# Cross attention on one core: turning the probabilities behind the keys, weighing two steps at once, half of the output weights resident

## What is computed

```python
q = (layernorm(x) @ Wq + bq).reshape(b, s, 16, 64)
k = (ctx @ Wk + bk).reshape(b, 2048, 16, 64)
v = (ctx @ Wv + bv).reshape(b, 2048, 16, 64)
logits = einsum('bshd,bShd->bhsS', q, k) / sqrt(64)
weights = softmax(logits, axis=-1)
x = x + einsum('bhsS,bShd->bshd', weights, v).reshape(b, s, 1024) @ Wo + bo
```

## Time and profile before

| | |
|---|---|
| median of 3 runs | 1503.95 us (1503.4 to 1504.15) |
| the profiled execution, its own time | 1505.97 us |
| its span, first to last instruction | 1504.2 us |
| mean granted clock of TensorE | 0.978 |
| busy: PE / DVE / ACT / POOL | 96% / 49% / 33% / 12% |
| cross attention | from 12.35 us, PE's first matmul, to 1190 us |

### The profile page before, as it was taken

One profiled execution on the slowest core, in us unless ns is written; L12 is line 12 of the kernel. 1 busy time (PEld: TensorE's weight loads), 2 busy tenths in 40 slices (PEclk: granted clock), 3 DMA queues, 4 the chain that ended last, 5 costly groups with the idle time before them and its releaser, 6 DMA issues. The chain is left out here.

```text
span 1504.2 us, 22239 instructions
## 1 busy us (share of the span) xinstructions
PE 1449.8 (96%) x8564; PEld 1115.5 (74%) x8564; DVE 739.4 (49%) x1644; ACT 502.8 (33%) x1111; POOL 173.8 (12%) x150
## 2 busy tenths in 40 slices
PE   5999999999999999999999999999999599799999
PEld 4667777777777777777777777777777377588777
DVE  5335433463354336434533463354335555577679
ACT  3115421471153136413421471153124424321111
POOL 3211000130020003101000130020000112100012
PEclk9999999999999999999999999999999897899999
DMA  6511000140010003201000140010011130023300
GB/s 210 174 65 43 19 12 11 39 134 1 11 50 12 11 8 105 61 11 32 18 12 12 39 134 1 11 43 5 4 60 57 16 112 1 26 88 100 96 30 29
DMA packets 44359, 71.50 MB, mean 48 GB/s; under 512 B 8048, under 2 KB 16272, under 8 KB 43616
## 3 DMA queue, kind: packets, MB, share of 16 engines
q1 hardware_dynamic: 42608, 65.04, 14.1%
q0 software_dynamic: 1648, 5.04, 1.1%
HBM read 64.82 MB, written 5.24 MB: 47 GB/s over the span
## 5 line engine op out<-in xcount | busy, mean ns | idle before, releaser
L404 PE MATMUL b_ps<-b_ctxT,wk 128*128 128x512 f32 x1536 | 388.0, 401 | 0.0
L382 PE MATMUL b_ps<-wv,b_ctxT 128*128 128x512 f32 x1536 | 373.2, 401 | 12.4 <-DVE b_ctxT L582 12.4
L382 PEld LDWEIGHTS b_ps<-wv,b_ctxT 128*128 128x128 f32 x1536 | 289.4, 190 | 86.6 <-issue 20.9
L404 PEld LDWEIGHTS b_ps<-b_ctxT,wk 128*128 128x128 f32 x1536 | 279.9, 189 | 58.1 <-issue 1.5
L686 DVE TENSOR_SCALAR_CACHE_REDUCE b_prob<-b_ps 128x512 f32<-128x512 f32 x256 | 166.6, 688 | 309.4 <-PE b_ps L420 309.4
L553 ACT COPY b_pT<-b_ps 128x512 f32<-128x512 f32 x128 | 75.1, 587 | 539.0 <-PE b_ps L433 529.4
L595 DVE COPY b_V<-b_ps 128x512 f32<-128x512 f32 x128 | 88.4, 691 | 250.8 <-PE b_ps L382 250.8
L562 ACT ACTIVATE b_prob<-b_prob,b_negm 128x512 f32<-128x512 f32 x256 | 182.9, 719 | 2.2 <-DVE b_negm L692 2.2
L451 PE MATMUL b_ps<-b_pT,b_V 128*64 128x128 f32 x2048 | 145.5, 279 | 0.3 <-ACT b_pT L553 0.3
L451 PEld LDWEIGHTS b_ps<-b_pT,b_V 128*64 128x64 f32 x2048 | 110.3, 136 | 46.4 <-issue 45.9
L433 PE MATMUL b_ps<-ident,b_prob 128*128 128x128 f32 x1024 | 138.0, 278 | 6.5 <-ACT b_prob L562 6.4
(11 more groups left out here) (201 smaller groups left out, 1249.6 us busy)
## 6 DMA issues: line engine op xcount, KB each, us to landing
stage<-in_ctx SPq DMA_DIRECT2D x64, 256.0 KB, 2.9
stage<-in_Wk SPq DMA_DIRECT2D x30, 256.0 KB, 2.6
stage<-in_Wv SPq DMA_DIRECT2D x28, 256.0 KB, 3.2
b_q<-q_s SPq DMA_DIRECT2D x32, 128.0 KB, 3.0
w_rows<-in_self_w SPq DMA_DIRECT2D x4, 1024.0 KB, 5.0
w_tiles<-in_q_proj SPq DMA_DIRECT2D x16, 256.0 KB, 3.9
w_tiles<-in_k_proj SPq DMA_DIRECT2D x16, 256.0 KB, 3.4
w_tiles<-in_v_proj SPq DMA_DIRECT2D x16, 256.0 KB, 3.4
```

Source lines behind the costliest of these rows:

```text
L382: mm = nc.tensor.matmul(ps[:, bank], ctxT[:, a, k, n * P:(n + 1) * P], wv[:, w, k], start=m == 0, stop=m == len(terms) - 1)
L404: mm = nc.tensor.matmul(ps[:, bank], wk[:, i % 2, w, k], ctxT[:, a, k, s * BANK:(s + 1) * BANK], start=m == 0, stop=m == len(terms) - 1)
```

## The change

Cross attention alone is changed.

- In a step PE does K, then T, then S. W is made in even steps only, for w - 2 and w - 1 (w = t - 6), one behind the other. `pT` has six half buffers instead of two, so a copy waits for the weighing three steps back. The special order of the tail is gone.
- V moves two steps later, O one (within its step it stands where it stood), the value weights are split two steps later, the epilogue comes one step later.
- ACT exponentiates first in a step and copies T after it; DVE does its context chunks ahead of its copy of T.
- `wo` holds half of Wo (4 of 8 row blocks). SP loads the other half each time the group that used it is done: 8 loads of 1 MB in place of one of 2 MB.
- At the start ACT and DVE split the two key weights after x has been transposed instead of before the first value chunks; POOL adds the output bias after the last query product, and the raw tiles lie at other addresses.

```diff
-    LAG_EXP, LAG_WEIGH = 5, 6
+    LAG_EXP, LAG_TURN, LAG_WEIGH = 5, 6, 8
...
-                self.products[half * h + 3 + n // SB].append(("v", h, n))
+                self.products[half * h + 5 + n // SB].append(("v", h, n))
...
-                groups = [(at + 24, 0, 4), (at + 31, 4, 6), (at + 35, 6, 7), (at + 38, 7, 8)]
+                groups = [(at + 25, 0, 4), (at + 32, 4, 6), (at + 36, 6, 7), (at + 39, 7, 8)]
...
-        work += [(half * h - 8 + c, ("wv", h, c)) for h in range(1, self.HALVES) for c in range(C)]
+        work += [(half * h - 6 + c, ("wv", h, c)) for h in range(1, self.HALVES) for c in range(C)]
...
+        loads += [(half * k + (9 if k % 2 == 0 else 10), 2, k, ("wo", k)) for k in range(1, 2 * NB)]
...
-        wo = sb("wo", [P, NP, D])
+        wo = sb("wo", [P, HALF, D])
         pT_at = nc.sbuf_base
-        pT = sb("pT", [P, 2, 4, P])
+        pT = sb("pT", [P, SLOTS, 4, P])
...
+                elif item[0] == "wo":
+                    k = item[1]
+                    sp.wait_ge(o_psum, outs_of(k - 1)[-1] + 1)
+                    sp.dma_start(wo[:], Wo[:, k % 2 * HALF:(k % 2 + 1) * HALF]).then_inc(wo_in, 16)
```

PE:

```diff
             for t in range(LAST + 1):
-                w = t - G.LAG_WEIGH
-                if 0 <= w and t <= TOTAL:
-                    transpose_probs(w)
+                w = t - G.LAG_TURN
                 if t < TOTAL:
                     keys(t)
+                if 0 <= w < TOTAL:
+                    transpose_probs(w)
                 if 1 <= t <= TOTAL:
                     scores(t - 1)
-                if t >= TOTAL and w + 1 < TOTAL:
-                    transpose_probs(w + 1)
-                if 0 <= w < TOTAL:
-                    weigh(w)
+                if w >= 2 and w % 2 == 0:
+                    weigh(w - 2)
+                    weigh(w - 1)
```

ACT and DVE, start and steps:

```diff
-            for n in range(C, len(PRE)):
-                pre_split(n)
...
+                if item[0] == "x":
+                    for n in range(C, len(PRE)):
+                        pre_split(n)
...
-                    if w >= 1:
-                        act.wait_ge(pv_done, 2 * w - 1)
-                    nc.scalar.copy(pT[:, 0], ps[:, TB].rearrange("p (m t) -> p m t", m=4)).then_inc(te_done, 1)
...
+                    if 2 * w >= SLOTS:
+                        act.wait_ge(pv_done, 2 * w - SLOTS + 1)
+                    nc.scalar.copy(pT[:, 2 * w % SLOTS], ps[:, TB].rearrange("p (m t) -> p m t", m=4)).then_inc(te_done, 1)
...
-            for n in range(C, len(PRE)):
-                pre_rest(n)
...
+                    for n in range(C, len(PRE)):
+                        pre_rest(n)
...
+                for item in G.splits[t]:
+                    if item[0] == "ctx" and item[2] % 2 == 0:
+                        chunk_rest(item[1], item[2])
                 if 0 <= w < TOTAL:
```

More of the change, by code:

```diff
@@ L121, in __init__ @@
         self.TOTAL = NB * self.STEPS
-        self.LAST = self.TOTAL + self.LAG_WEIGH
+        self.LAST = self.TOTAL + 7
         self.HALVES = 2 * NB
@@ L186, in cross_attention @@
     QBUFS = 2
+    SLOTS = 6
     with ExitStack() as ctx:
@@ L220, in cross_attention @@
         xnT = at("xnT", [P, C, TOK], prob_at + 4 * C * HW + 4 * NB * D)
-        raw = at("raw", [P, len(PRE), BANK], wo_at)
-        bo_b = at("bo_b", [P, D], wo_at + 4 * len(PRE) * BANK)
+        raw_v = at("raw_v", [P, C, BANK], wo_at)
+        raw_k = at("raw_k", [P, 2, BANK], pT_at + 16 * QBUFS * TOK // 2)
+        bo_b = at("bo_b", [P, D], attn_at)
+        raw = [raw_v[:, c] for c in range(C)] + [raw_k[:, i] for i in range(2)]
         qhi = at("qhi", [P, QBUFS, TOK], pT_at, F32R)
@@ L251, in chunk_lo, with outs_of @@
                 eng.wait_ge(clo_odd, NC // 2 * b + (n + 1) // 2)
+        def outs_of(k):
+            return [n for n, (_, b, first, _) in enumerate(G.outs) if 2 * b + first // HALF == k]
         def weight_lo(eng, item):
@@ L297, in _ @@
             for i in range(2):
-                sp.dma_start(raw[:, C + i], Wk[i]).then_inc(pre_in[C + i], 16)
+                sp.dma_start(raw[C + i], Wk[i]).then_inc(pre_in[C + i], 16)
             for n in range(4, NC):
@@ L303, in _ @@
             sp.wait_ge(pre_lo, len(PRE))
-            sp.wait_ge(xbo_done, NB)
-            sp.dma_start(wo[:], Wo).then_inc(wo_in, 16)
+            sp.dma_start(wo[:], Wo[:, :HALF]).then_inc(wo_in, 16)
             for i in range(2):
@@ L334, in _ @@
                 chunk_rest(0, n)
[L335 to L338, removed]
             for j in range(NP):
@@ L344, in _ @@
                     pool.dma_start(q_s[l, j], src[:, j % QBUFS].bitcast(F32)).then_inc(q_stored[j % QBUFS], 16)
+            pool.wait_ge(bo_in, 16)
+            pool.wait_ge(ln[5], NB)
+            for b in range(NB):
+                nc.gpsimd.tensor_tensor(xs[:, b], xs[:, b], bo_b[:], ALU.add).then_inc(xbo_done, 1)
             for t in range(LAST + 1):
@@ L388, in out_product @@
                 bank = bank_free(item)
-                pe.wait_ge(wo_in, 16)
+                pe.wait_ge(wo_in, 16 * (2 * b + first // HALF + 1))
                 pe.wait_ge(attn_done, NP * b + last)
                 for i in range(first, last):
-                    mm = nc.tensor.matmul(ps[:, bank], attnT[:, i], wo[:, i], start=i == first, stop=i == last - 1)
+                    mm = nc.tensor.matmul(ps[:, bank], attnT[:, i], wo[:, i % HALF], start=i == first, stop=i == last - 1)
                 mm.then_inc(o_psum, 1)
@@ L450, in weigh @@
                         col = (i % HALF * 2 + h) * HD
-                        mm = nc.tensor.matmul(ps[h * HD:(h + 1) * HD, OB, 0:P], V[:, c, col:col + HD], pT[:, half, m],
+                        mm = nc.tensor.matmul(ps[h * HD:(h + 1) * HD, OB, 0:P], V[:, c, col:col + HD], pT[:, (2 * w + half) % SLOTS, m],
                                               start=c == 0, stop=c == NC - 1)
@@ L529, in _ @@
             split_hi(("ctx", 0, 3))
-            for n in range(C, len(PRE)):
-                pre_split(n)
             act.wait_ge(bq_in, 16)
             for item in G.first:
-                if item[0] == "v" and item[2] + 4 < NC:
+                if item[0] == "x":
+                    for n in range(C, len(PRE)):
+                        pre_split(n)
+                elif item[0] == "v" and item[2] + 4 < NC:
                     split_hi(("ctx", 0, item[2] + 4))
@@ L647, in _ @@
             for t in range(LAST + 1):
-                w, e = t - G.LAG_WEIGH, t - 1
-                if w >= SB and w % SB == 0:
+                w, e = t - G.LAG_TURN, t - 1
+                if w > SB and w % SB == 1:
                     i = w // SB - 1
@@ L657, in _ @@
                     dve.wait_ge(o_free, i + 1)
+                    if i == 0:
+                        dve.wait_ge(xbo_done, NB)
                     if i >= NP and i % HALF == 0:
@@ L665, in _ @@
                     dve.wait_ge(t_psum, 2 * w + 2)
-                    if w >= 1:
-                        dve.wait_ge(pv_done, 2 * w)
-                    nc.vector.tensor_copy(pT[:, 1], ps[:, TB + 1].rearrange("p (m t) -> p m t", m=4)).then_inc(to_done, 1)
+                    if 2 * w >= SLOTS:
+                        dve.wait_ge(pv_done, 2 * w - SLOTS + 2)
+                    nc.vector.tensor_copy(pT[:, (2 * w + 1) % SLOTS], ps[:, TB + 1].rearrange("p (m t) -> p m t", m=4)).then_inc(to_done, 1)
                     if s == SB - 1:
@@ L676, in _ @@
                         dve.wait_ge(rinv_done, i + 1)
-                for item in G.splits[t]:
-                    if item[0] == "ctx" and item[2] % 2 == 0:
-                        chunk_rest(item[1], item[2])
                 if 0 <= e < TOTAL:
```

15 lines of the change are left out of this document (8 added, 7 removed).

## The result

The kernel after takes 1487.86 us in the median of 4 runs (1486.79 to 1492.95), the kernel before 1503.68 beside it (4 runs): a ratio of 0.9908 (0.9889 to 0.9926). In a second comparison it took 1489.99 (4 runs), ratio 0.9903 (0.9885 to 0.9920). It is faster by 15 to 16 us by the medians, 14 to 15 by the ratios; 10.7 were forecast, and the range held it.

What follows compares the result with a forecast made beforehand. PE, busy 96% of the span, was taken as the bound. Steps -3.6, tail -6.1, start -4.3 and reload +3.3 sum to -10.7: 1505.97 becomes 1495.3, the median 1493.3 us; range 1486.5 to 1500.

Steps and rivals of the forecast that it cites:

- Steps: Cross attention's step pairs in the new order: .04 us gained 46 times, .13 gained 14 times with V, together 3.6.
- Rival (a): In the steps, all changes of form cost alike, five instead of six per pair: -9.6 us for -3.6, 1487.3; chance 0.10.
- Waits in short steps: In steps without W, S's low keys are ready at 6.87 and wanted at 8.61, 1.7 us left: cost 0.
- rival (d): In every short step S waits for the low keys, as DVE's chain hangs on the previous S: 1517 us; chance 0.05.
- Reload: Context reloaded three times: DVE's chunks now precede T's copy, scores and low keys, making S .95 us late: +3.3 in all.
- Rival (b): Reload costs 9 us instead of 3.3, late copies of T piling up into the next step: 1499; chance 0.13.
- Tail: From K(127) to the last O: 26.0 us instead of 30.38, and one T and W move behind K(127); gain 6.1.
- Start: Before X's third batch, DVE is freed from POOL's additions and key weights: gain 3.5 to 5.7 us, taken as 4.3.
- Rival (c): Both ends only move their waits: tail gains 3, start 1, reload costs 6: 1502.4 us; chance 0.08.
- SP's queue: SP's eight Wo loads wait for an O last in its step; PE uses them 15 steps on: cost 0.

Runs made afterwards that it cites:

- the chunks' order: Kernel after, with DVE subtracting context chunks cast before the key copy between its T copy and scores, the rest behind the low keys: 1486.58 us, ratio 0.9881 to the kernel before.

## Why the prediction was right, point by point

- **Steps, forecast -3.6, measured -5.8.** The 4.59 less from K(0) to K(127) hold 2.95 of waits in the reload, and 1.75 of T and W that moved behind K(127): 4.59 + 2.95 - 1.75. The new side of the term was right: K 2.90 for 2.89, the pair 11.40. What was mis-sized is the old side: the sum took 5.72 for every plain step, and two of four take 5.75. Four plain steps take 23.03 for 23.17, .07 a pair where .04 was forecast. Four steps with V take 67.73 for 67.99, and the keys behind the last of them 2.79 for 2.90: .18 a pair for .13. 46 x .07 and 14 x .18 make 5.7 of the 5.8. The steps with O, for which the sum had nothing, have next to nothing.
- **Rival (a)** asked for 9.6 in this place. The runs show why it is half right. Taking one change of form away is worth .15 a pair, nearly what equal shares gave (.16), but the order with T before S costs .08 of it again, or .12 against the shortest old steps, which only the rows told. The rule of the Trainium skill (TensorEngine Tiling (Array Packing), section Key Properties), that changing the tiling mode drains TensorE, agrees with the .15. That the sides of a change differ in price the section doesn't say. The rows do: K before T takes 2.79 where V, of the same form, stands before it, the shortest K of the kernel, and 2.90 where S or W does, so what it loses is lost on that side and not towards T.
- **Waits in short steps, 0 forecast.** None stood there outside the reload; rival (d) fell.
- **Reload, +3.3 forecast, +2.95 measured**, one S late in each, by .97 to 1.01 (.95 forecast), and by the forecast's chain: third cast, subtraction, T, scores, low keys. Rival (b), with 9, fell, though the second profile lost 1.0 more in two further steps. The experiment that undid this order took the waits away.
- **Tail, -6.1 forecast, -6.3 measured** (4.54 in the tail, and the 1.75 that moved into it): 25.85 from K(127) to the last O, for 26.0, and S(127) late by 1.14 for 1.1. The buffers alone give 3.97 of the 4.54 without any new order, by taking away ACT's wait for the weighing. What the prediction did not see is that weighing in pairs, good for the steps, holds the tail back by 1.5.
- **Start, -4.3 forecast, -5.2 measured.** The ends were 3.5 with the low clock and 5.7 without. With the clock held the profiles have 5.2 and 5.1 (78.8 and 78.7 to K(0)). In the kernels with the chunks' order it fell for 6.8, K(0) came after 81.4, and the start gave 2.6, less than the lower end. DVE's normalising took 2.89 for 4.85, as estimated. The other half of POOL's share was not foreseen: the subtractions beside it had been slow too. The forecast called them 3.46 for two and put their gain down to their being moved; without POOL they take 1.32.
- **Outside the sum, 0 forecast, 2.6 to 5.2 by the profiles.** Self attention had less time at the low clock in both profiles of the kernel after. The sum took the part behind the last O as fixed, though the page of before shows the clock at 7 to 9 tenths there. Other kernels of the new order took as long behind the last O as the kernel before (315.11 and 316.03 for 315.55), so the cause is open, and what the medians hold of it (some 1.5 us, 15.8 less 14.3 and 14.9 less 13.2) is luck as far as the sum goes.
- **Rival (c)** fell: tail and start gave what they promised or more.
- **A claim that held by luck.** The prediction set SP's queue at 0, for the eight loads of Wo in the steps, and did not look at the first load, which in the old layout waits for the additions that the change moves. The kernel after is safe there, since its bias no longer lies where Wo goes; its start alone, in the old layout, lost 8.84 us of PE in that queue. The new layout, or else the queries loaded first, is what makes the new start usable.

The forecast's sum was too small by 3.6 in cross attention (-10.7 for -14.3), 2.2 of it in the steps, .9 at the start, and the rest in tail and reload.

## What to carry to other kernels

Price a change of form by its neighbours, each side by itself, from rows in which that neighbourhood occurs; a count of changes gave 9.6 us here, where 5.8 came. Price the old side with the same care: 5.72 for a step that takes 5.75 every second time was the largest part of the miss in the steps. When work is moved later, follow every queue that waits for it: additions of 5 us on an idle engine held up a DMA queue, and the loads behind it cost more than the move gave. Where an engine waits for another that only waits for a buffer, count buffers before reordering: six half buffers alone took 4 us out of the tail. And price a new order where the steps end as well: the pairs that gave .15 each in the steps cost 1.5 in the tail.

## What was not expected of the hardware

- POOL's additions slow DVE beside them. DVE's four normalisings took 4.85 us beside POOL and 2.89 without it, two subtractions 3.46 and 1.32, while POOL's own four took 6.03, and 5.04 once they had been moved. The Trainium skill (GPSIMD Engine Reference, section Specifications) says that GpSimd shares its way to SBUF with VectorE and that they contend with VectorE's instructions of two SBUF inputs or in a two-port mode; the two subtractions, with two inputs in SBUF, agree with it. Whether the normalising ran in such a mode no run here shows.
- At the start TensorE's clock fell in some executions and held in others. It held in the two profiles of the kernel after, where PE stood idle for 2.07 and 1.89 us before X's third batch, and fell in the six other profiles with the additions moved, where the idle time was 2.81 to 3.12. The kernel after was idle for less because its first value chunks took 1.1 us longer (10.9 us from the first matmul to X, for 9.8 with the chunks' order), though both have the same start. How long the low clock lasted is not told by that idle time: after 3.12 it was 3.4 us where W stands in every step, after 3.11 it was 6.8 with the chunks' order. From the first matmul to K(0) that makes 78.7 and 78.8 with the clock held, 79.9 with 3.4 and 81.4 with 6.8 us of the low clock: as much as the smaller terms of the sum.
